# The first 80 microseconds of a two-layer kernel: Wv's first slice as float32 between the x tiles, transposes one product ahead

## The reference, cut to what matters

```python
normed = (x - mu) * rsqrt(var + 1e-05) * norm_g + norm_b       # x: 4096 x 1024 per core
hv = silu(normed @ W_h + b_h);  v, gate = hv[:, :2048], hv[:, 2048:]
qk = silu(normed @ W_qk + b_qk)                                # 128 wide
heads = qk[:, None, :] * qk_gamma + qk_beta                    # quad_q, lin_q, quad_k, lin_k
attn = square(relu(quad_q @ quad_k.T / 256 + rel_bias))        # within groups of 256 tokens
lin_kv = lin_k.T @ v / 4096                                    # over all 4096 tokens
out = (gate * (attn @ v + lin_q @ lin_kv)) @ W_o + b_o + x
x = layernorm(x + out)
x = layernorm(x + relu(x @ W1 + b1) @ W2 + b2)
```

## Time and profile before

| | us |
|---|---|
| median of 3 runs | 1749.39 (1748.23 to 1775.63) |
| the profiled execution, its own time | 1749.52 |
| span of its slowest core (core 0, which the rows show) | 1748.0 |
| spans of the eight cores | 1745.3 to 1748.0 |
| TensorE busy | 1703.2 (97%) |
| VectorE, ScalarE, GpSimd busy | 548.0, 436.3, 316.4 |

### The profile page before, as it was taken

The page is one execution under the profiler, slowest core; times in us unless marked ns, Lnnn a source line. Parts: engine busy times, 40 slices in busy tenths (PEclk is TensorE's granted clock), DMA queues, the critical chain, the costliest instruction groups (busy, mean ns, idle before and its releaser), DMA issues.

```text
span 1748.0 us, 23816 instructions; the slowest of 8 cores (1745.3 to 1748.0 us)
## 1 busy us (share of the span) xinstructions
PE 1703.2 (97%) x8320; PEld 805.3 (46%) x8320; DVE 548.0 (31%) x947; ACT 436.3 (25%) x684; POOL 316.4 (18%) x494
## 2 busy tenths in 40 slices
PE   3899999999999999999999999999999999999998
PEld 1344444445445445445444444444444444444443
DVE  3466654354454454454302012020120211202102
ACT  2344444312212213213230311303113022040220
POOL 3444442022322322312301001010010000100001
PEclk9899999999999999999999999999999999999999
DMA  7857762637467477454870112012220121110201
GB/s 176 181 141 187 190 166 79 175 112 155 141 164 152 143 169 144 144 139 123 191 217 37 61 37 84 12 44 67 37 63 22 49 73 37 50 36 25 73 1 48
DMA packets 93523, 180.94 MB, mean 104 GB/s; under 512 B 39648, under 2 KB 43744, under 8 KB 93408
## 3 DMA queue, kind: packets, MB, share of 16 engines
q1 hardware_dynamic: 78288, 149.77, 27.0%
q0 software_dynamic: 15120, 29.63, 12.5%
HBM read 139.53 MB, written 69.47 MB: 120 GB/s over the span
## 4 chain that ended last, share of the span: by engine, by line
PE 96%; DMA 1%; DVE 1%; POOL 1%; issue 1%; ACT 0%; SPq 0%; POOLq 0%; DVEq 0%; ACTq 0%
PE pb L725 25%; PE pb L702 25%; PE pb L668 13%; PE pb L634 13%; PE pb L569 12%; PE pb L656 3%; PE pb L650 2%; PE pb L579 2%; DMA xs<-x 1%; PE pb L539 1%; PE pb L550 1%; POOL n0s L451 0%; DVE nfm L815 0%; DVE bnst L227 0%; DVE bnst L228 0%
## 5 line engine op out<-in xcount | busy, mean ns | idle before, releaser
L702 PE MATMUL pb<-xfm,w1s 128*128 128x512 bf16 x2048 | 443.3, 379 | 0.0
L796 ACT ACTIVATE h<-pb,prms 128x512 bf16<-128x512 f32 x256 | 175.9, 687 | 653.2 <-PE pb L702 653.2
L702 PEld LDWEIGHTS pb<-xfm,w1s 128*128 128x128 bf16 x2048 | 200.4, 98 | 241.6
L929 DVE TENSOR_TENSOR xr<-pb,xr 128x512 f32<-128x512 f32 x64 | 44.2, 691 | 715.4 <-PE pb L725 715.4
L569 PE MATMUL pb<-wvs,nfm 128*128 128x512 bf16 x1024 | 248.8, 387 | 0.1
L634 PE MATMUL pb<-nfm,wgs 128*128 128x512 bf16 x1024 | 240.6, 379 | 0.0
L725 PE MATMUL pb<-w2a,h 128*128 128x512 bf16 x1024 | 231.5, 379 | 0.0
L668 PE MATMUL pb<-wos,gated 128*128 128x512 bf16 x1024 | 224.6, 379 | 0.0
L237 POOL TENSOR_SCALAR veps<-mv 128x1 f32<-128x1 f32 x96 | 21.8, 227 | 1002.2 <-DVE mv L232 1001.2
L725 PEld LDWEIGHTS pb<-w2a,h 128*128 128x128 bf16 x1024 | 100.2, 98 | 120.8
L569 PEld LDWEIGHTS pb<-wvs,nfm 128*128 128x128 bf16 x1024 | 100.3, 100 | 117.2 <-issue 12.9
(11 more groups left out here) (59 smaller groups left out, 1001.8 us busy)
## 6 DMA issues: line engine op xcount, KB each, us to landing
v_sp<-vst SPq DMA_DIRECT2D x32, 512.0 KB, 8.1
vb<-v_sp SPq DMA_DIRECT2D x32, 512.0 KB, 7.1
xr<-x SPq DMA_DIRECT2D x32, 512.0 KB, 13.1
x_sp<-xr SPq DMA_DIRECT2D x32, 512.0 KB, 3.0
xr<-x_sp SPq DMA_DIRECT2D x32, 512.0 KB, 8.0
out<-xr SPq DMA_DIRECT2D x32, 512.0 KB, 2.6
xt<-x SPq DMA_DIRECT2D x24, 512.0 KB, 5.7
w_sp<-w POOLq DMA_DIRECT2D x32, 256.0 KB, 13.8
```

The lines of the kernel that those rows point to most:

```text
L702: mm = te.matmul(pb[4 + n % 2][:], w1[:, w_:w_ + 128], xfm[:, x_:x_ + 512], start=(c == 0), stop=(c == 7))
L796: sc.activation(h1[:, ci * 512:(ci + 1) * 512], pb[4 + n % 2][:], AF.Relu, bias=prm[:, P_B1 + ci:P_B1 + ci + 1]).then_inc(S["s_h1"], 1)
```

## The change

Wv's first slice now comes as float32 in eight pieces of 256 KB on SP's queue (`load_wv_first` into a new buffer `wvf`), four between x tiles 0 and 1 and four between x tiles 1 and 2; ScalarE casts pieces 0 to 5 and VectorE pieces 6 and 7 (`cast_wv`), and unit 0 waits for the pieces one by one. GpSimd issues no load before tile 1 is normalized: Wqk's load follows tile 1, the other slices follow tiles 4, 6 and 7. `prm` and `ident` are issued by ScalarE. The slots become: tile 0 in slot 0, tiles 1 and 2 in slot 1, tile 3 in slot 2, and so on to tile 7 in slot 6; VectorE takes the statistics of tile t+1 ahead of its eviction of tile t; `qk(0)` is in slot 4 and uses PSUM bank 0, `qk(1)` in slot 8, `lk_transpose(1)` in slot 11. The bias rows arrive already repeated for 128 partitions, so their loads read a row for each partition. GpSimd's last instruction of `rs_chain` becomes `shift`, which is no longer run in the last stage. The x tiles 8 to 10 wait once, for tile 5.

```diff
 def t_slot(t):
     if t < 8:
-        return (0, 0, 0, 1, 2, 4, 5, 6)[t]
+        return (0, 1, 1, 2, 3, 4, 5, 6)[t]
 def stat_slot(t):
-    return (0, 1, 2, 3, 4, 8, 11, 14)[t - 3] if t < 11 else t_slot(t - 3)
+    return (9, 11, 13)[t - 8] if t < 11 else t_slot(t - 3)
 def qk_slot(b):
-    return (3, 9)[b] if b < 2 else 16 * b
+    return (4, 8)[b] if b < 2 else 16 * b
 def lkt_slot(b):
-    return (7, 12)[b] if b < 2 else 16 * b + 4
+    return (7, 11)[b] if b < 2 else 16 * b + 4
...
-    bv_h = din("bv", [HID])
+    bv_h = din("bv", [128, HID])
...
+    def shift(gp, k):
+        j = k % 8
         wt(gp, "s_rs", k + 1)
-        gp.tensor_scalar(nmr[:, j:j + 1], mv[:, m:m + 1], rstd[:, j:j + 1], -1.0, ALU.mult, ALU.mult).then_inc(S["s_nm"], 1)
+        gp.tensor_scalar(nmr[:, j:j + 1], mv[:, 2 * j:2 * j + 1], rstd[:, j:j + 1], -1.0,
+                         ALU.mult, ALU.mult).then_inc(S["s_nm"], 1)
...
+        def load_wv_first(c):
+            sy.dma_start(out=wvf[:, c * 512:(c + 1) * 512], in_=wv_h[0, :, c * 512:(c + 1) * 512]).then_inc(d_wvf[c], 16)
         load_x_first(0)
-        sy.dma_start(out=prm[:], in_=prm_h[:, :]).then_inc(d_prm, 16)
-        sy.dma_start(out=ident[:], in_=id_h[:, :]).then_inc(d_id, 16)
+        for c in range(4):
+            load_wv_first(c)
         load_x_first(1)
+        for c in range(4, 8):
+            load_wv_first(c)
         load_x_first(2)
         load_bv(0)
...
+        load_bv(1)
+        wt(sy, "s_n0", 6)
         load_x(8)
-        load_bv(1)
+        load_bv(2)
         load_x(9)
-        load_bv(2)
+        load_bv(3)
         load_x(10)
-        load_bv(3)
...
-        load_wv(0)
-        gp.dma_start(out=wqk[:], in_=wqk_h[:, :]).then_inc(d_wqk, 16)
...
         for t in range(NT):
             norm0(t)
-            if t in (3, 5, 7):
-                load_wv((t - 1) // 2)
-            if t % 4 == 1 and t >= 5:
+            if t == 1:
+                gp.dma_start(out=wqk[:], in_=wqk_h[:, :]).then_inc(d_wqk, 16)
+            if t in (4, 6, 7):
+                load_wv((1, 0, 2, 3)[t - 4])
+            if t == 6 or t % 4 == 1 and t >= 9:
                 head_lk(t // 4 - 1)
...
             for c in range(8):
+                if u == 0:
+                    wt(te, "s_wca", min(c + 1, 6))
+                    wt(te, "s_wcd", c - 5)
                 mm = te.matmul(pb[4 + u % 2][:], nfm_tok(t, c), wv[:, s * 4096 + c * 512:s * 4096 + (c + 1) * 512],
...
+        sc.dma_start(out=prm[:], in_=prm_h[:, :]).then_inc(d_prm, 16)
+        sc.dma_start(out=ident[:], in_=id_h[:, :]).then_inc(d_id, 16)
         sc.wait_ge(S["s_initp"], 1)
         sc.activation(mhalf[:, 1:2], mhalf[:, 0:1], AF.Silu)
+        def cast_wv(c):
+            sc.wait_ge(d_wvf[c], 16)
+            sc.copy(wv[:, c * 512:(c + 1) * 512], wvf[:, c * 512:(c + 1) * 512]).then_inc(S["s_wca"], 1)
+        for c in range(4):
+            cast_wv(c)
...
                 nfm_evict(t)
+                if t == 0:
+                    cast_wv(4)
+                    cast_wv(5)
...
-        for t in range(3):
-            stats_a(t)
-            if t == 0:
-                scale_heads()
+        stats_a(0)
+        scale_heads()
         for u in range(NU):
             for t in tiles_at(u):
+                if 1 <= t < 7:
+                    stats_a(t + 1)
                 nfm_evict(t)
-            for t in range(3, NT):
+                if t == 0:
+                    stats_a(1)
+                    cast_wv(6)
+                    cast_wv(7)
+            for t in range(8, NT):
                 if stat_slot(t) == u:
                     stats_a(t)
```

More of the change, by code:

```diff
@@ L94, in build_program @@
     prm_h = din("prm", [128, P_N])
-    bv_h = din("bv", [HID])
-    bo_h = din("bo", [DM])
-    b2_h = din("b2", [DM])
+    bv_h = din("bv", [128, HID])
+    bo_h = din("bo", [128, DM])
+    b2_h = din("b2", [128, DM])
     wv_h = din("wv", [4, 128, 4096])
@@ L138, in build_program @@
     o = 135168
+    wvf = at("wvf", 98304, 4096, F32)
     n0s = at("n0s", 16384, 8 * 1024, BF16)
@@ L189, in build_program @@
     d_x = sems("d_x", 3)
+    d_wvf = sems("d_wvf", 8)
     d_wv = sems("d_wv", 4)
@@ L206, in build_program @@
     d_out = sems("d_out", 4)
-    names = ("s_init s_initp s_bn s_mv s_ve s_rs s_nm s_n0 s_T s_nfa s_nfd s_vmm s_vad s_vsi s_lkv s_qk s_qks "
+    names = ("s_init s_initp s_wca s_wcd s_bn s_mv s_ve s_rs s_nm s_n0 s_T s_nfa s_nfd s_vmm s_vad s_vsi s_lkv s_qk s_qks "
              "s_lk s_hd s_lkT s_lkt "
@@ L229, in bn_stats @@
         wt(ve, "s_bn", 2 * k + 2)
-        wt(ve, "s_nm", k - 7)
+        if k < 2 * NT + 8:
+            wt(ve, "s_nm", k - 7)
+        else:
+            wt(ve, "s_no3", k - 2 * NT - 7)
         m = (k % 8) * 2
@@ L272, in load_bv @@
             sy.dma_start(out=bv[:, s * 512:(s + 1) * 512],
-                         in_=bass.AP(bv_h.tensor, s * 512, [[0, 128], [1, 512]])).then_inc(d_bv[s], 16)
+                         in_=bv_h[:, s * 512:(s + 1) * 512]).then_inc(d_bv[s], 16)
+        def load_wv_first(c):
+            sy.dma_start(out=wvf[:, c * 512:(c + 1) * 512], in_=wv_h[0, :, c * 512:(c + 1) * 512]).then_inc(d_wvf[c], 16)
         load_x_first(0)
-        sy.dma_start(out=prm[:], in_=prm_h[:, :]).then_inc(d_prm, 16)
-        sy.dma_start(out=ident[:], in_=id_h[:, :]).then_inc(d_id, 16)
+        for c in range(4):
+            load_wv_first(c)
         load_x_first(1)
+        for c in range(4, 8):
+            load_wv_first(c)
         load_x_first(2)
@@ L285, in load_x @@
             i, n = ring(t - 8, 3)
-            if t < 11:
-                wt(sy, "s_n0", 2 * t - 12)
-            else:
+            if t >= 11:
                 wt(sy, "s_n0", t - 2)
@@ L349, in emit_sync @@
             load_xr(t)
-        sy.dma_start(out=bo[:], in_=bass.AP(bo_h.tensor, 0, [[0, 128], [1, 1024]])).then_inc(d_bo, 16)
-        sy.dma_start(out=b2[:], in_=bass.AP(b2_h.tensor, 0, [[0, 128], [1, 1024]])).then_inc(d_b2, 16)
+        sy.dma_start(out=bo[:], in_=bo_h[:, :]).then_inc(d_bo, 16)
+        sy.dma_start(out=b2[:], in_=b2_h[:, :]).then_inc(d_b2, 16)
         for i in range(3):
@@ L447, in norm0 @@
             x_landed(gp, t)
+            shift(gp, t)
             wt(gp, "s_nm", t + 1)
@@ L450, in norm0 @@
                 wt(gp, "s_T", t - 1)
-            gp.tensor_scalar(n0_tile(t), x_tile(t),
-                             rstd[:, j:j + 1], nmr[:, j:j + 1], ALU.mult, ALU.add).then_inc(S["s_n0"], 1)
+            gp.tensor_scalar(n0_tile(t), x_tile(t), rstd[:, j:j + 1], nmr[:, j:j + 1],
+                             ALU.mult, ALU.add).then_inc(S["s_n0"], 1)
         def head_lk(b):
@@ L479, in emit_gpsimd @@
             for k in range(pieces_before(t), pieces_before(t + 1)):
+                if k == 16:
+                    wt(gp, "s_wca", 6)
+                    wt(gp, "s_wcd", 2)
                 if k < 16:
@@ L518, in emit_gpsimd @@
                 i = t % 4
+                if t >= 8:
+                    wt(gp, "s_x2f", t - 7)
+                shift(gp, NT + t)
                 if t == 0:
@@ L543, in qk @@
             wt(te, d_wqk, 16)
-            n = 1 + max(t for t in range(NT) if t_slot(t) <= qk_slot(b))
+            n = 4 if b == 0 else 1 + max(t for t in range(NT) if t_slot(t) <= qk_slot(b))
             wt(te, "s_nfa", n)
@@ L549, in qk @@
                 o_ = b * 4096 + c * 512
-                mm = te.matmul(pb[7][:], wqk[:, c * 128:(c + 1) * 128], nfm[:, o_:o_ + 512],
+                mm = te.matmul(pb[0 if b == 0 else 7][:], wqk[:, c * 128:(c + 1) * 128], nfm[:, o_:o_ + 512],
                                start=(c == 0), stop=(c == 7))
@@ L562, in v_unit @@
             if t == 0:
-                te.wait_ge(d_wv[s], 16 * 2)
+                if s:
+                    te.wait_ge(d_wv[s], 16 * 2)
             if s == 0:
@@ L576, in linkv_unit @@
             wt(te, "s_lkt", t // 4 + 1)
+            if u == 0:
+                wt(te, "s_qks", 1)
             o_ = ((u // 4) % 3) * 2048 + (u % 4) * 512
@@ L748, in emit_scalar @@
                 wt(sc, "s_hd", b)
-                sc.activation(qkf[:], pb[7][:], AF.Silu, bias=prm[:, P_BQK:P_BQK + 1]).then_inc(S["s_qks"], 1)
+                sc.activation(qkf[:], pb[0 if b == 0 else 7][:], AF.Silu, bias=prm[:, P_BQK:P_BQK + 1]).then_inc(S["s_qks"], 1)
             q, j = divmod(u, 4)
@@ L833, in attn, with cast_wv @@
             ve.scalar_tensor_tensor(attnT[:, a_:a_ + 512], sims[:], 0.0, sims[:], ALU.max, ALU.mult).then_inc(S["s_att"], 1)
-        for t in range(3):
-            stats_a(t)
-            if t == 0:
-                scale_heads()
+        def cast_wv(c):
+            ve.wait_ge(d_wvf[c], 16)
+            ve.tensor_copy(wv[:, c * 512:(c + 1) * 512], wvf[:, c * 512:(c + 1) * 512]).then_inc(S["s_wcd"], 1)
+        stats_a(0)
+        scale_heads()
         for u in range(NU):
             for t in tiles_at(u):
+                if 1 <= t < 7:
+                    stats_a(t + 1)
                 nfm_evict(t)
```

(9 more changed lines are left out.)

## The result

The changed kernel took 1773.97 us (1772.85 to 1776.71), the kernel before 1749.29 (1748.23 to 1775.63): a ratio of 1.0145, 95% interval 1.0122 to 1.0168. Forecast were 1742.9 and a range of 1738.0 to 1750.0.

A forecast was written before the change was run, and what follows sets the result against it. It took TensorE's idle time at the start as all the change could touch. Product 14 starting at 73.7 instead of 80.30 gave 1749.5 - 6.6 = 1742.9 us, range 1738.0 to 1750.0.

The forecast's parts named there:

- The failing step: TensorE's idle time: 36.5 of 44.8 us lie in the first 100, so a wait removed there is kept.
- The wait grows from 4.1 to about 6.0: At `lk_transpose(1)`, moved to slot 11 with product 11 after it: TensorE's wait was to grow by this much, in us.
- rival 1: Start: identity as late as before, transposes 0 at 11.5, 1.7 later; 5.0 us gained, 1744.5; chance 0.13.
- The loads: SP's queue at the start: 350 GB/s from x0 at 5.0, bringing x1 at 9.5, x2 at 14.0, bias at 14.8.
- Rival 2: Float32 loads hold up the bias: at 200 GB/s it lands at 22.0; 0.4 us gained or 1751.9; chance 0.08.
- The loop: Eviction, statistics, GpSimd, transposes and products of the first tiles: 4.2 to 4.7 us a tile instead of 7.
- Rival 3: The loop keeps its 7 us a tile; start worth 4.3 less 2, 2.3 us gained, 1747.2; chance 0.08.
- The sum: `lk_transpose(1)` at 64.7 plus 8.96 puts product 14 at 73.7 instead of 80.30, 6.6 us earlier.
- low-clock price of a product: A product of eight matmuls on TensorE: 2.96 us at granted clock 0.50, against 1.89 at full clock.

The follow-up runs named there:

- a_fill: The changed kernel with 28 matmuls that nobody reads added in the wait before `lk_transpose(1)`: 1746.22 us.
- a_nostall: The changed kernel with the statistics of tiles 8 and 9 in slots 7 and 8 instead of 9 and 11: 1742.6 us, ratio 0.9963.

## Why the prediction was wrong, point by point

**The failing step** is in the first paragraph: that "a wait taken away there is gained for good: TensorE hardly stops later, so nothing there can swallow the gain". It counted idle time alone. From 100 us on TensorE is as busy as foretold, but its clock isn't fixed. The wait at 62 to 68 us decides whether a pair of cores may fall to 0.81 for 160 us after it, at 27.7 us a time. With the wait left out or filled 0 of 140 pairs were hit; with 4.1 us 48 of 216, with 6.05 to 6.1 us 33 of 82. The prediction's own rows showed the first half of it, the fall to 0.50 behind the wait, and priced it as a product of 3.62 us. The 1749.5 that the forecast starts from is a time without a pair hit, and that was luck: in the later jobs only 12 of 48 executions of the kernel before were like it. With a pair hit the kernel lies outside the range, which ended at 1750.0. And one of the three times of before was 1775.63, 26 us above the others; the text gave the range and asked nothing of it.

**"The wait grows from 4.1 to about 6.0"**: measured 6.05. The step was right, and its price was wrong by 27.7 us on the cores hit.

**The identity, rival 1.** The first transposes no longer wait for it; they wait for x0, which lands at 5.8 in the median (5.4 before). They start at 10.6, not at 9.84.

**The loads** were the mis-sized term. This is the windows view of core 5 of the changed kernel: busy time of PE, PEld, DVE, ACT and POOL, granted clock, DMA share, GB/s.

```profile
3.00:10.00 7.00, 0.00 (x0) 0.00 (x0) 1.97 (x11) 0.53 (x2) 1.05 (x3) 1.00 0.90 198
10.00:20.00 10.00, 5.66 (x23) 2.50 (x24) 4.05 (x9) 5.13 (x10) 4.44 (x6) 1.00 1.00 344
```

The 350 GB/s of the earlier trace rows holds only from 10 us on; before that it is 198 (198 to 252 over the eight cores). Rival 2's 200 was near the right number for the first part. On VectorE's timeline it reads so:

```profile
13.69 0.68 DVE L231 BATCH_NORM_STATS2 bnst<-xs 128x6 f32<-128x512 f32 x1
...
16.97 0.43 DVE L881 CAST wvs<-wvf 128x512 bf16<-128x512 f32 x1 [1.69 <-DMA wvf<-wv]
17.61 1.12 DVE L881 CAST wvs<-wvf 128x512 bf16<-128x512 f32 x1 [0.22 <-DMA wvf<-wv]
20.13 0.69 DVE L912 TENSOR_TENSOR vtmp<-pb,bvs 128x512 f32<-128x512 f32 x1 [1.39 <-DMA bvs<-bv]
20.74 0.68 DVE L231 BATCH_NORM_STATS2 bnst<-xs 128x6 f32<-128x512 f32 x1
```

Both casts and the bias add wait for their loads here. In the medians of the cores: statistics 1 at 13.7 (forecast 11.96), the last cast's end at 18.2 (14.9), the bias add at 19.5 (15.8), statistics 2 at 20.1 (16.5; before 19.5). From the 5.0 us of the working to 19.5 the 3.41 MB make 235 GB/s. The whole path is 3.7 us late from here.

**The loop** was right: statistics 2 at 20.1, 7 at 44.2, 4.8 us a tile (forecast 4.2 to 4.7). It makes good what the start lost. What it replaced was not 7 us a tile throughout: before, statistics 2 to 7 ran from 19.5 to 48.0, 5.7 a tile, and only tiles 2 to 5 were 7 apart. Rival 3, a loop that keeps its 7 us, is out, though its 2.3 us are near what was gained.

**The sum.** In the medians of the cores `lk_transpose(1)` starts at 67.6 (forecast 64.7; before 72.4), and product 11 then comes behind it. Product 14 starts at 75.75 (before 78.7), so the path is 2.95 ahead, not 6.6. The difference of 3.65 has two parts. Against the 73.7 of the forecast product 14 is 2.05 late, which is what is left of the 3.7 that the loads cost. The other 1.6 is the starting point: the sum took product 14 of before from core 0, 80.30, where the median core has 78.7. A smaller slip is the low-clock price of a product, 2.96: on core 0 the clock was back at 1.00 from 35 us on, within that product, and the 3.62 of the earlier trace rows is the price at the low clock. Of the 2.95 the spans of cores not hit show 1.5; where the other 1.4 went stays open. It is less than the spread of the cores of one execution (5 us).

**What the wait costs by itself.** Taking it out gains 6.9 us on the changed kernel (1744.5 to 1737.6) and 6.2 on the kernel before (1746.0 to 1739.8), beside the pairs. Filling it gains 2.4 (a_fill), which is what the low clock behind it cost. The change gained at the start and left 6 us in its longest wait.

**Left open.** Why some pairs are hit and others not. In the nine profiled pairs that were hit, both cores stood at 0.50 for 6.8 us, the two came back to 1.00 within 0.2 to 1.9 us of each other (each in the time of its own trace), and 0.81 began 3.6 to 4.8 us after the later one. In twelve of nineteen that were not hit the two returns were 2.3 to 6.1 apart; but seven pairs at most 1.5 apart also stayed at 1.00, so this isn't the whole condition. With the wait of 4.1 us half of the profiled cores (8 of 16) stood at 0.50 for only 3.4 us, with 6.05 to 6.1 every core for 6.8: that fits the two rates, but no run tests it. Nor is every return from 0.50 enough: in the start, until some 54 us, the clock of most cores falls to 0.50 and comes back in the versions without the wait too (in a_nostall core 2 was at 0.50 from 50 to 52 us and at 1.00 from 54 on), and no pair was hit. Nor does the length of the wait alone set how often: 6.7 us at 170 us hit 6 of 48 pairs, 6.05 at 62 us 25 of 60. What it is in the chip that grants 0.81 to two cores was not tried.

## What to carry to other kernels

Read the granted clock beside the idle time: here a stop of TensorE of 6 us in the dense stretch cost 6.9 us, and on a pair of cores it often cost 160 us at 0.81, another 27.7, so the longest wait left in the dense part comes first, above a faster start. Where it can't be taken away, filling it with matmuls kept the clock (a_fill). When one of a few given times lies 26 us above the others, look at the clock of each core before forecasting a change of 7, and size the first loads by a row of those first microseconds. Take the starting point of a sum from the median core, not from one.

## What the runs showed of the hardware that was not expected

**A clock between the levels, on a pair of cores.** 0.81 for 160 us, some 4 us behind a return from 0.50, then 1.00 again under the same load, on both cores of a pair, in the profile above with the other two of the die at 1.00. The Trainium skill, TensorE: Matmul & The Clock Gate, Seeing it yourself, tells of a current limiter that takes a whole die to 13/16 of full clock when three of its cores run dense, and holds it while the load lasts. The level agrees (0.81), and a whole die at it is on record too: in one execution of the kernel before (2108.32 us) the four cores of a die ran at a mean clock of 0.813 to 0.816. The pairs don't fit: most cores are not held there, though all eight run dense for some 1650 us, cores 6 and 7 kept 1.00 (538 matmuls in 100 us) beside 4 and 5 (449), and the 0.81 ended at 237 us under the same load. Here the measurement decides; whether one limiter makes both is not shown.

**VectorE's cast beside GpSimd.** On core 5 the cast of 128x512 from float32 to bf16 that started at 16.97, just ahead of GpSimd's normalization (16.99 to 18.46), took 0.43 us; the one that started inside it, at 17.61, took 1.12 and ended 0.27 after it. GpSimd's timeline shows that it lost too, 1.47 instead of 1.19:

```profile
16.99 1.47 POOL L467 TENSOR_SCALAR n0s<-xs,rstd,nmr 128x1024 bf16<-128x1024 f32 x1 [0.18 <-POOL nmr L253]
...
24.07 1.19 POOL L467 TENSOR_SCALAR n0s<-xs,rstd,nmr 128x1024 bf16<-128x1024 f32 x1 [0.18 <-POOL nmr L253]
```

The Trainium skill, SBUF — State Buffer, SBUF: two separate sides, says that the two engines share a port pair, and that a GpSimd instruction or a VectorE one in a two-port mode, whichever starts first, holds it for the whole instruction while the other is blocked. These rows agree in kind; in which mode the casts ran no row shows. The forecast had 0.63 to 0.69 a cast, and their sum came out close (1.55).
